# Probability-value products in four column quarters of the array, transposed back, in the second layer of a two-layer conditioned attention kernel

## The chip, the cores and the metric

The kernel runs on one core of one Trainium2 chip, in one launch. The metric is the device time of that launch in microseconds (us): all 64 sequences through both layers.

## The reference, cut to what matters

Sequences of 128 tokens and 512 features pass through two layers. The change is in the second, a softmax attention with 16 heads of 32 features, followed by a norm that a condition scales and shifts, a SiLU, an output product and a residual sum:

```python
xn = layer_norm(x, norm_w, norm_b)
q = (xn @ q_w + q_b).reshape(Bx, Tx, H, -1)          # H = 16, 32 features a head
k = (xn @ k_w + k_b).reshape(Bx, Tx, H, -1)
att = jnp.einsum('bnhl,bmhl->bnmh', q, k)
att = jax.nn.softmax(att + (1.0 - mask) * -1000000.0, axis=2)
v = ((xn @ v_w + v_b) * src_mask[:, :, None]).reshape(Bx, Tx, H, -1)
y = jnp.einsum('bnmh,bmhl->bnhl', att, v).reshape(Bx, Tx, Dx)
h = layer_norm(y, sb_norm_w, sb_norm_b) * (1.0 + scale) + shift
return x + (jax.nn.silu(h) @ out_w + out_b)
```

## The kernel before

The kernel is written for the engines directly: each engine has its own program, in the order in which the code writes it, and semaphores join them. `layer0` runs first (the other layer's attention), then `layer1`, which is the reference's second layer. `layer1` takes the sequences in 32 pairs, and each engine's `body(i, ...)` is one turn of a loop: it does the front part of pair i (projections, keys' and queries' scores, row maxima) and the back part of pair i-1 (weights, probability-value products, norm, gate, output product). So TensorE (PE), whose order is written by hand with `woven` (one step of each of two lists in turn), always has work of two pairs at hand. The eight PSUM banks are shared by name: `W_BANKS`, `Y_BANKS`, `Z_BANKS`, `O_BANKS`, `X_BANKS`, `S_BANKS`, `V_BANKS`, `QK_BANKS`.

The steps that the change and the prediction touch, in one turn of PE:

- `projected` (L439 to L441): keys, then queries; each feature block is 12 matmuls of 256 columns. Inputs are split into a high and a low part, so three matmuls stand for one product.
- `weight_scores` (L1417): scores again with the row maxima subtracted, into banks 4 to 7; ScalarE (ACT) makes `prob` from them with an exponential (`exps`, L1291). `prob[:, b, h, :]` has the keys on the partitions and the queries along the columns.
- `mixed` (L1427): for each of 16 heads `prob` is the stationary operand (128 columns) and `v` the moving one, 33 columns: 32 features and a column of ones, whose result is the sum of the probabilities. Both are float32, and the profile shows each such product as two weight loads and two matmuls. The result `y` has queries on partitions, as the norm wants it. In the profile's names it is `bank<-v,prob`.
- `end_outputs` (VectorE, DVE: L1169, L1174, L1179, L1182): reciprocal of the sums, product into `z`, statistics. GpSimd (POOL) makes the reciprocal deviation (L1073), `end_norm` (L1196) finishes `z`.
- `value_rows` (L430 to L432, 128x512, `xT`): 12 matmuls of 512 columns a sequence; `z_transposed` (L1376), `x_transposed` (L1366): 128x128 transposes of `z` and of the next pair's `xn`, which `x_high` (ACT, L1276) and `x_low` (DVE, L1143) split.
- `gate`, `tanh`, `end_silu`, `h_high`, `low_part` (ACT L1301, L1307, DVE L1201, ACT L1311, DVE L1205): from the transposed `z` to the operand of `out_rows` (L430 to L432 with `h_hi`, `h_lo`: 12 matmuls of 512 columns a sequence).
- `scores` (L1443): 16 matmuls a sequence into banks 0 to 3, in eight steps of two, from `stack`, in which SyncE's (SP) 24 DMAs of 128 KB (`restack`, L1034) put the high and low parts of keys and queries; `maxima` (DVE, L1160) takes the row maxima of each bank, `shift_row` (L1453) turns them, `shift_out` (ACT, L1315, L1317) sends them into `stack`.

`layer0` has one product that is laid out in column halves already, L922: two heads of 64 features share the array, each with 65 moving float32 columns. `tile_position=(0, DH * r)` there names the first column of the part of the array that the product uses.

Of the kernel before, what the change touches and what calls it, by code (L numbers as in the profile page):

```python
# [12 lines left out]
P = 128  # L13
PAIR = 2
# [941 lines left out]
def layer1(nc, ctx, sem, sb, ps, x1_d, out, xr, x_in, w_hi, w_lo, ident, bias_all, qk_bias,  # L956
# [4 lines left out]
    DV = DH + 1  # L961
# [11 lines left out]
    v = sb(ctx, "v1", [P, PAIR, H, DV])  # L973
# [27 lines left out]
        "shift0", "shift1", "w_ps", "prob", "y_ps", "p_sum", "y", "y_stats", "y_var", "y_var_eps", "y_rstd", "z",  # L1001
# [18 lines left out]
    def _(sp):  # L1020
        sp.wait_ge(s["rows_preset"], 1)

        def restack(i, first):
# [21 lines left out]
            sp.wait_ge(s["qk_lo"], seq(2 * C, i, 2 * C))  # L1045
            rows(0, Q_LO, 1)
# [77 lines left out]
    def _(dve):  # L1124
# [21 lines left out]
        def qk_low(i, n):  # L1146
            for c in range(C):
# [16 lines left out]
        def end_outputs(prev, b):  # L1164
            banks = Y_BANKS[b]
            dve.wait_ge(s["y_ps"], seq(PAIR, prev, b + 1))
            for j in range(2):
                a = ps[banks[j]][:, 0:HY * DV].rearrange("p (h d) -> p h d", h=HY)
                last = nc.vector.reciprocal(p_sum[:, b, HY * j:HY * j + HY], a[:, :, DH])  # L1169
            last.then_inc(s["p_sum"], 1)  # L1170
            dve.wait_ge(s["p_sum"], seq(PAIR, prev, b + 1))
            for j in range(2):
                a = ps[banks[j]][:, 0:HY * DV].rearrange("p (h d) -> p h d", h=HY)
                last = nc.vector.tensor_tensor(  # L1174
                    z[:, b, HY * DH * j:HY * DH * (j + 1)].rearrange("p (h d) -> p h d", h=HY), a[:, :, 0:DH],
                    p_sum[:, b, HY * j:HY * j + HY].unsqueeze(2).broadcast_to([P, HY, DH]), ALU.mult)
# [7 lines left out]
        def values(i, b, first):  # L1184
            dve.wait_ge(s["v_bias"], seq(1, i, 1))
            dve.wait_ge(s["v_ps"], seq(PAIR, i, b + 1))
            if not first:

                dve.wait_ge(s["y_ps"], seq(PAIR, i - 1, b + 1))
# [27 lines left out]
        nc.vector.memset(v[:], 1.0).then_inc(s["preset"], 1)  # L1217
# [6 lines left out]
        def body(i, first, more, last):  # L1224
            qk_low(i, 1)
            if not last:
                row_stats(i + 1, (i + 1) % RING)
            qk_low(i, 0)
            if not first:
                end_outputs(i - 1, 0)  # L1230
            if not last:
                norm(i + 1, (i + 1) % RING)
            if not first:
                end_norm(i - 1, 0)
                end_outputs(i - 1, 1)
# [16 lines left out]
            if not first:  # L1252
                end_add(i - 1, (i - 1) % RING, 0)
            maxima(i, 1, (2,))
            if not last:
                x_low(i + 1, 1)
            maxima(i, 1, (3, 0, 1))
# [15 lines left out]
    def _(act):  # L1273
# [13 lines left out]

        def exps(prev, b):
            for j in range(C):
# [3 lines left out]
                                     ACT.Exp).then_inc(s["prob"], 1)  # L1293

# [28 lines left out]
        def body(i, first, more, last):  # L1323
# [9 lines left out]
            if not first:  # L1333
                gate(i - 1, 0)
                tanh(i - 1, 0)
            if not first:
                h_high(i - 1, 0)
            if not first:
                gate(i - 1, 1)
                tanh(i - 1, 1)  # L1340
                h_high(i - 1, 1)
            if not last:
                x_high(i + 1, 0)
                x_high(i + 1, 1)
# [5 lines left out]
        exps(NP - 1, 1)  # L1350
        for b in range(PAIR):
            gate(NP - 1, b)
            tanh(NP - 1, b)
# [4 lines left out]
    def _(pe):  # L1358
# [62 lines left out]
        def mixed(prev, b):  # L1421


            pe.wait_ge(s["prob"], seq(PAIR * C, prev, C + 2 * (b + 1)))
            for h in range(H):
                j, a = h // HY, h % HY
                last = nc.tensor.matmul(ps[Y_BANKS[b][j]][:, a * DV:(a + 1) * DV], prob[:, b, h, :], v[:, b, h, :],  # L1427
                                        start=True, stop=True)
                yield
            last.then_inc(s["y_ps"], 1)  # L1430
# [26 lines left out]
        def body(i, first, more, last):  # L1457
# [12 lines left out]
            run(projected(i, 0, (0, 1)))  # L1470
            if first:
                run(projected(i, 0, (2, 3)))
            else:
# [61 lines left out]
```

## Time and profile before

| | |
|---|---|
| three runs | 2375.79, 2377.82, 2378.31 us, median 2377.82 |
| profiled execution | 2378.15 us; its span 2376.0 us |
| busy share of the span | PE 97%, weight loads (PEld) 87%, DVE 61%, ACT 35%, POOL 24% |
| one turn of `layer1`'s loop | 39.72 us (1619.98 to 1659.70) |

Times in the profile are counted from the span's start. PE's rows give the start of a matmul and a modelled duration that includes its way through the array, so that rows overlap; what a matmul costs the stream is the distance from its start to the next one's. PEld is the load of a stationary operand, which runs beside the matmul ahead of it. A row's bracket is the idle time ahead of it and what ended it.

### The profile page before, as it was taken

What the parts mean: (1) busy time and instruction counts of PE and PEld (TensorE: products, weight loads), DVE (VectorE), ACT (ScalarE), POOL (GpSimd) and SP (SyncE); (2) the same over time, 40 slices, a digit from 0 to 9 for tenths busy, and PEclk for the clock granted to TensorE, in tenths of its full rate; (3) what the DMA queues carried; (4) which work ended last, traced back from release to release, by engine and by line L of the source; (5) the groups of instructions that cost most, each with busy time, mean ns of one, the idle gap of its engine ahead of it and who ended that gap; (6) DMA issues with size and microseconds to landing.
All of it is one profiled execution on the core that took longest, in us unless ns stands there. A gap on an engine that the chain in (4) does not pass through costs nothing.

```text
span 2376.0 us, 44691 instructions
## 1 busy us (share of the span) xinstructions
PE 2316.1 (97%) x16182; PEld 2061.4 (87%) x16182; DVE 1459.6 (61%) x3249; ACT 822.1 (35%) x1893; POOL 574.3 (24%) x847
## 2 busy tenths in 40 slices
PE   7999999999999999969999999999999999999997
PEld 5888888888888888848898989898989898989896
DVE  4677777777777777653646465656565646464643
ACT  2233333333333333322333333333333333333332
POOL 0333333333333333231212121212122212222110
PEclk9999999999999999968999999999999999999997
DMA  7200000000001000004353535353434343434441
GB/s 244 80 36 35 35 35 35 35 35 35 35 35 35 33 34 35 32 32 109 89 124 90 124 90 122 92 121 94 120 95 118 96 117 94 118 95 118 97 109 41
DMA packets 90932, 187.14 MB, mean 79 GB/s; under 512 B 18708, under 2 KB 29394, under 8 KB 90904
## 3 DMA queue, kind: packets, MB, share of 16 engines
q1 hardware_dynamic: 88856, 186.23, 29.4%
q10 hardware_dynamic: 2048, 0.53, 0.1%
q8 instruction: 18, 0.29, 0.1%
q14 instruction: 10, 0.08, 0.0%
HBM read 51.81 MB, written 33.69 MB: 36 GB/s over the span
## 4 chain that ended last, share of the span: by engine, by line
PE 47%; ACT 4%; DVE 3%; issue 1%; SPq 1%; DMA 0%; DVEq 0%; POOL 0%; POOLq 0%
PE bank L1427 7%; PE bank L439 6%; PE bank L441 6%; PE bank L440 6%; PE bank L1417 5%; PE bank L431 4%; PE bank L432 4%; PE bank L430 4%; PE bank L1443 3%; ACT g L1301 2%; PE bank L1376 1%; PE bank L1366 1%; DVE top L1160 1%; DVE hs L1201 1%; ACT th L1307 1%
## 5 line engine op out<-in xcount | busy, mean ns | idle before, releaser
L439 PE MATMUL bank<-xT_hi,w_hi 128*128 128x256 f32 x1536 | 447.1, 291 | 2.6 <-DVE xT_lo L1143 1.4
L440 PE MATMUL bank<-xT_lo,w_hi 128*128 128x256 f32 x1536 | 447.6, 291 | 0.0
L441 PE MATMUL bank<-xT_hi,w_lo 128*128 128x256 f32 x1536 | 444.9, 290 | 0.0
L1152 DVE SCALAR_TENSOR_TENSOR parts<-bank,qk_bias,parts 128x256 fp32r<-128x256 f32 x256 | 112.2, 480 | 433.0 <-ACT parts L1284 433.0
L1427 PEld LDWEIGHTS bank<-v,prob 128*128 128x128 f32 x2048 | 317.6, 195 | 12.7
L430 PE MATMUL bank<-w_hi,xT_hi 128*128 128x512 f32 x768 | 322.2, 420 | 0.0
L432 PE MATMUL bank<-w_lo,xT_hi 128*128 128x512 f32 x768 | 322.1, 419 | 0.0
L431 PE MATMUL bank<-w_hi,xT_lo 128*128 128x512 f32 x768 | 319.9, 417 | 0.0
L439 PEld LDWEIGHTS bank<-xT_hi,w_hi 128*128 128x128 f32 x1536 | 292.4, 190 | 4.7 <-DVE xT_lo L1143 1.8
L440 PEld LDWEIGHTS bank<-xT_lo,w_hi 128*128 128x128 f32 x1536 | 293.8, 191 | 1.8
L441 PEld LDWEIGHTS bank<-xT_hi,w_lo 128*128 128x128 f32 x1536 | 293.4, 191 | 0.0
L1427 PE MATMUL bank<-v,prob 128*128 128x33 f32 x2048 | 293.3, 251 | 0.0
L430 PE MATMUL bank<-w_hi,h_hi 128*128 128x512 f32 x512 | 220.3, 430 | 3.6 <-DVE h_lo L1205 3.6
L1443 PEld LDWEIGHTS bank<-stack 98*128 98x128 f32 x1024 | 183.1, 194 | 45.1 <-DVE top L1160 23.0
L431 PE MATMUL bank<-w_hi,h_lo 128*128 128x512 f32 x512 | 215.4, 421 | 0.0
L432 PE MATMUL bank<-w_lo,h_hi 128*128 128x512 f32 x512 | 211.5, 413 | 0.0
L1284 ACT ACTIVATE parts<-bank,qk_bias 128x256 fp32r<-128x256 f32 x256 | 107.3, 470 | 288.5 <-PE bank L441 288.5
L787 ACT ACTIVATE k_exp<-bank,k_neg 128x128 f32<-128x128 f32 x256 | 72.8, 369 | 370.8 <-DVE k_neg L672 368.6
L1443 PE MATMUL bank<-stack 98*128 98x128 f32 x1024 | 178.8, 265 | 9.5 <-DMA stack<-parts 5.7
L1301 ACT ACTIVATE g<-bank,gains 128x128 f32<-128x128 f32 x256 | 96.2, 457 | 234.2 <-PE bank L1376 234.2
L1160 DVE TENSOR_REDUCE top<-bank 128x4 f32<-128x512 f32 x256 | 169.6, 682 | 7.5 <-PE bank L1443 7.3
L432 PEld LDWEIGHTS bank<-w_lo,xT_hi 128*128 128x128 f32 x768 | 145.1, 189 | 29.9
(163 smaller groups left out, 4078.6 us busy)
## 6 DMA issues: line engine op xcount, KB each, us to landing
stack<-parts SPq DMA_DIRECT2D x768, 128.0 KB
xr<-in_x SPq DMA_DIRECT2D x32, 512.0 KB, 3.5
x_between_layers<-x SPq DMA_DIRECT2D x64, 256.0 KB, 2.0
xr<-x_between_layers SPq DMA_DIRECT2D x32, 512.0 KB, 3.6
out<-y_out SPq DMA_DIRECT2D x64, 256.0 KB, 2.0
w_emb<-in_L_cond_W_emb SPq DMA_DIRECT2D x4, 1024.0 KB, 10.2
w_emb<-in_L_cond_emb_w SPq DMA_DIRECT2D x4, 1024.0 KB, 5.2
raw<-in_L_cond_Wq SPq DMA_DIRECT2D x1, 1024.0 KB, 5.4
```

What stands on the lines that cost most here:

```text
L430: yield nc.tensor.matmul(bank[:, :], a_hi[:, c, b, :], w_hi[:, m, c, :], start=(c == 0), stop=False)
L431: yield nc.tensor.matmul(bank[:, :], a_lo[:, c, b, :], w_hi[:, m, c, :], start=False, stop=False)
L432: yield nc.tensor.matmul(bank[:, :], a_hi[:, c, b, :], w_lo[:, m, c, :], start=False, stop=(c == C - 1))
L439: yield nc.tensor.matmul(dst, w_hi[:, m, c, fs], a_hi[:, c], start=(first and c == 0), stop=False)
L440: yield nc.tensor.matmul(dst, w_hi[:, m, c, fs], a_lo[:, c], start=False, stop=False)
L441: yield nc.tensor.matmul(dst, w_lo[:, m, c, fs], a_hi[:, c], start=False, stop=(c == C - 1))
L1152: nc.vector.scalar_tensor_tensor(parts[:, LO[n], c].rearrange("p b t -> p (b t)"), ps[QK_BANKS[n][c // 2]][:, at:at + PAIR * P], qk_bias[: ...
L1160: nc.vector.tensor_reduce(top[:, b, :].rearrange("p (a c) -> p a c", c=C)[:, :, j], ps[S_BANKS[j]][:, :].rearrange("p (h t) -> p h t", h=H ...
L1301: last = nc.scalar.activation(g[:, b, c, :], ps[Z_BANKS[b]][:, c * P:(c + 1) * P], ACT.Identity, scale=gains[:, 0, c, b:b + 1], bias=gains ...
L1417: last = nc.tensor.matmul(ps[W_BANKS[j]][:, a * P:(a + 1) * P], stack[0:K_SHIFTED, 1, a, j, b, :], stack[0:K_SHIFTED, 0, a, j, b, :], star ...
L1427: last = nc.tensor.matmul(ps[Y_BANKS[b][j]][:, a * DV:(a + 1) * DV], prob[:, b, h, :], v[:, b, h, :], start=True, stop=True)
L1443: last = nc.tensor.matmul(ps[S_BANKS[j]][:, a * P:(a + 1) * P], stack[0:K_SCORE, 0, a, j, b, :], stack[0:K_SCORE, 1, a, j, b, :], start=Tr ...
```

## The change

1. `mixed`: `v` (32 columns, no column of ones) becomes the stationary operand and `prob` the moving one, 128 columns. The four heads of a group go to the four column quarters of the array (`tile_position=(0, DH * a)`), and their results, features on partitions, fill one bank of a sequence. The sums come from 16 further products with `one_col`, a stationary operand whose column c is ones and whose other columns are zeros, so that the sums of 16 heads land in 16 rows of the second bank.
2. `copy_yT` (ACT) copies both results from PSUM into `prob`'s own place, and `turned` (PE) transposes them back in five 128x128 transposes a sequence. `end_outputs` then reads one bank of y and the sums from the other, with one reciprocal and one product in place of two each.
3. PE's order: all query blocks, then `mixed` of both sequences back to back, then `value_rows` woven with `turned`, then `z_transposed(0)`, the next pair's `x_transposed`, and all eight steps of the first sequence's scores; only behind them `z_transposed(1)` and the first `out_rows`, woven with the second sequence's scores. The second `out_rows` stands alone at the end.
4. ACT's order: `x_high` of the next pair stands ahead of `h_high(0)`, and four DMAs of the low query rows move from SP to ACT (`query_low_rows`). DVE's order: `values(0)` ahead of `end_norm(0)`, silu and low part of both sequences among the maxima.

```diff
-    v = sb(ctx, "v1", [P, PAIR, H, DV])
+    v = sb(ctx, "v1", [P, PAIR, H, DH])
+    one_col = sb(ctx, "one_col", [P, C, DH])
...
             rows(0, Q_HI, 0)
             rows(0, Q_HI, 2)
-            sp.wait_ge(s["qk_lo"], seq(2 * C, i, 2 * C))
-            rows(0, Q_LO, 1)
...
         def end_outputs(prev, b):
             banks = Y_BANKS[b]
             dve.wait_ge(s["y_ps"], seq(PAIR, prev, b + 1))
-            for j in range(2):
-                a = ps[banks[j]][:, 0:HY * DV].rearrange("p (h d) -> p h d", h=HY)
-                last = nc.vector.reciprocal(p_sum[:, b, HY * j:HY * j + HY], a[:, :, DH])
-            last.then_inc(s["p_sum"], 1)
+            nc.vector.reciprocal(p_sum[:, b, :].rearrange("p (c a) -> p c a", c=C),
+                                 ps[banks[1]][:, 0:P].rearrange("p (a r) -> p r a", a=HC)[:, 0:C, :])\
+                .then_inc(s["p_sum"], 1)
...
         def body(i, first, more, last):
-            qk_low(i, 1)
+            qk_low(i, 1, range(C))
             if not last:
                 row_stats(i + 1, (i + 1) % RING)
-            qk_low(i, 0)
-            if not first:
-                end_outputs(i - 1, 0)
+            qk_low(i, 0, range(C))
             if not last:
                 norm(i + 1, (i + 1) % RING)
             if not first:
+                end_outputs(i - 1, 0)
+            values(i, 0, first)
+            if not first:
                 end_norm(i - 1, 0)
                 end_outputs(i - 1, 1)
-                end_silu(i - 1, 0)
-            values(i, 0, first)
-            if not first:
-                end_norm(i - 1, 1)
-                low_part(i - 1, 0)
             values(i, 1, first)
             maxima(i, 0, (0,))
             if not first:
-                end_silu(i - 1, 1)
+                end_norm(i - 1, 1)
+                end_silu(i - 1, 0)
             maxima(i, 0, (1,))
             if not first:
-                low_part(i - 1, 1)
+                low_part(i - 1, 0)
             maxima(i, 0, (2,))
             if not last:
                 x_low(i + 1, 0)
             maxima(i, 0, (3,))
...
+        def query_low_rows(i):
+            act.wait_ge(s["qk_lo"], seq(2 * C, i, 2 * C))
+            for a in range(HC):
+                act.dma_start(f32(stack[DH:2 * DH, 0, a]),
+                              f32(parts[DH * a:DH * a + DH, Q_LO])).then_inc(s["stack"], 16)
...
+        def copy_yT(prev, b):
+
+            act.wait_ge(s["yT_ps"], seq(2 * PAIR, prev, 2 * b + 2))
+            nc.scalar.activation(prob[:, b, 0:C, :].rearrange("p h t -> p (h t)"), ps[Y_BANKS[b][0]][:, :],
+                                 ACT.Copy).then_inc(s["yT"], 1)
+            nc.scalar.activation(prob[:, b, C, :], ps[Y_BANKS[b][1]][:, 0:P], ACT.Copy).then_inc(s["yT"], 1)
...
         def mixed(prev, b):
 
-
             pe.wait_ge(s["prob"], seq(PAIR * C, prev, C + 2 * (b + 1)))
-            for h in range(H):
-                j, a = h // HY, h % HY
-                last = nc.tensor.matmul(ps[Y_BANKS[b][j]][:, a * DV:(a + 1) * DV], prob[:, b, h, :], v[:, b, h, :],
-                                        start=True, stop=True)
+            for c in range(C):
+                for a in range(HC):
+                    last = nc.tensor.matmul(ps[Y_BANKS[b][0]][DH * a:DH * a + DH, c * P:(c + 1) * P],
+                                            v[:, b, HC * c + a, :], prob[:, b, HC * c + a, :], start=True, stop=True,
+                                            tile_position=(0, DH * a))
+            last.then_inc(s["yT_ps"], 1)
+            for c in range(C):
+                for a in range(HC):
+                    last = nc.tensor.matmul(ps[Y_BANKS[b][1]][DH * a:DH * a + DH, 0:P], one_col[:, c, :],
+                                            prob[:, b, HC * c + a, :], start=(c == 0), stop=(c == C - 1),
+                                            tile_position=(0, DH * a))
+            last.then_inc(s["yT_ps"], 1)
...
-            run(projected(i, 0, (0, 1)))
+            run(projected(i, 0, range(C)))
+            if not first:
+                mixed(i - 1, 0)
+                mixed(i - 1, 1)
+            woven(value_rows(i, 0), () if first else turned(i - 1, 0))
+            woven(value_rows(i, 1), () if first else turned(i - 1, 1))
...
```

In PE's program, where the products stood between the matmuls of the query blocks and of the values in the turn before (end of the query blocks; the row with x6 holds the first sequence's last five and the second's first):

```order
L1427 MATMUL bank<-v,prob 128x33
L440 MATMUL bank<-xT_lo,w_hi 128x256
L441 MATMUL bank<-xT_hi,w_lo 128x256
L1427 MATMUL bank<-v,prob 128x33 x6
L430 MATMUL bank<-w_hi,xT_hi 128x512
L1427 MATMUL bank<-v,prob 128x33
L431 MATMUL bank<-w_hi,xT_lo 128x512
L1427 MATMUL bank<-v,prob 128x33
```

now 64 products stand in one block (L1445 those with `v`, L1451 the sums, L1462 `turned`):

```order
L441 MATMUL bank<-xT_hi,w_lo 128x256
L1445 MATMUL bank<-prob,v 32x128 [waits l1_prob]
L1445 MATMUL bank<-prob,v 32x128 x15
L1451 MATMUL bank<-prob,one_col 32x128 x16
L1445 MATMUL bank<-prob,v 32x128 [waits l1_prob]
L1445 MATMUL bank<-prob,v 32x128 x15
L1451 MATMUL bank<-prob,one_col 32x128 x16
L430 MATMUL bank<-w_hi,xT_hi 128x512 [waits l1_qk_lo]
L1462 MATMUL bank<-ident,prob 128x128 [waits l1_yT]
L431 MATMUL bank<-w_hi,xT_lo 128x512
L1462 MATMUL bank<-ident,prob 128x128
```

The products have left the rows between the projections; the transposes have come in among the values.

Later in the same turn, at the join of values, scores and output product, PE's program was:

```order
L1427 MATMUL bank<-v,prob 128x33
L431 MATMUL bank<-w_hi,xT_lo 128x512
L1376 MATMUL bank<-ident,z 128x128 x4
L1427 MATMUL bank<-v,prob 128x33 x5
...
L432 MATMUL bank<-w_lo,xT_hi 128x512
L1376 MATMUL bank<-ident,z 128x128 x4
L1443 MATMUL bank<-stack 128x128 x4
L430 MATMUL bank<-w_hi,h_hi 128x512
```

and is now (L1395 `z_transposed`, L1385 `x_transposed`, L1478 `scores`):

```order
L432 MATMUL bank<-w_lo,xT_hi 128x512
L1395 MATMUL bank<-ident,z 128x128 [waits l1_z]
L1395 MATMUL bank<-ident,z 128x128 x3
L1385 MATMUL bank<-ident,xn 128x128 [waits l1_y,l1_xn]
L1385 MATMUL bank<-ident,xn 128x128 x3
L1385 MATMUL bank<-ident,xn 128x128 [waits l1_y,l1_xn]
L1385 MATMUL bank<-ident,xn 128x128 x3
L1478 MATMUL bank<-stack 128x128 [waits l1_stack]
...
L1395 MATMUL bank<-ident,z 128x128 [waits l1_z]
L1395 MATMUL bank<-ident,z 128x128 x3
L430 MATMUL bank<-w_hi,h_hi 128x512 [waits l1_h_lo]
```

The first sequence's z is transposed behind the values of both sequences, no longer in the middle of the first's, and between it and the first output matmul stand eight transposes of the next x and 16 score matmuls.

ACT's program between the query parts and the end of the gates was (L1284 `qk_high`):

```order
L1284 ACTIVATE parts<-bank,qk_bias 128x256 x4
L1301 ACTIVATE g<-bank,gains 128x128 x4
L1307 ACTIVATE th<-g 128x512
L1311 ACTIVATE h_hi<-hs 128x4x128
L1301 ACTIVATE g<-bank,gains 128x128 x4
L1307 ACTIVATE th<-g 128x512
L1311 ACTIVATE h_hi<-hs 128x4x128
L1276 ACTIVATE xT_hi<-bank 128x4x128 x2
```

and is now:

```order
L1284 ACTIVATE parts<-bank,qk_bias 128x256 x4
L1304 ACTIVATE prob<-bank 128x512
L1306 ACTIVATE prob<-bank 128x128
L1291 DMA stack<-parts 32x1024 x4
L1304 ACTIVATE prob<-bank 128x512
L1306 ACTIVATE prob<-bank 128x128
L1314 ACTIVATE g<-bank,gains 128x128 x4
L1320 ACTIVATE th<-g 128x512
L1276 ACTIVATE xT_hi<-bank 128x4x128 x2
L1324 ACTIVATE h_hi<-hs 128x4x128
```

The copies and the four DMAs are new ahead of the gate, and the next x's high parts stand between the tanh and the high part of h.

## Rows read from the trace of the kernel before

**Rows 1.** The page: the span and the number of instructions.

```profile
span 2376.0 us, 44691 instructions
```

**Rows 2.** Windows, one turn: length, busy PE, PEld, DVE, ACT, POOL, clock, DMA.

```profile
1619.98:1659.70 39.72, 39.60 (x291) 36.30 (x290) 22.00 (x49) 14.29 (x32) 8.08 (x13) 1.00 0.44 107
```

**Rows 3.** Waits of PE's weight loads, 1400 to 2200: total, times, longest.

```profile
PEld bank L1443 <- DVE top L1160: 14.9, 40, 0.4
...
PEld bank L430 <- DVE h_lo L1205: 4.6, 20, 0.2
```

**Rows 4.** Timeline of PE: start, duration, instructions merged where alike.

```profile
1637.56 1.42 PE L1427 MATMUL bank<-v,prob 128*128 128x33 f32 x12
1638.81 0.48 PE L430 MATMUL bank<-w_hi,xT_hi 128*128 128x512 f32 x1
...
1639.27 0.48 PE L431 MATMUL bank<-w_hi,xT_lo 128*128 128x512 f32 x1
...
1645.69 0.40 PE L431 MATMUL bank<-w_hi,xT_lo 128*128 128x512 f32 x1
1645.93 0.39 PE L432 MATMUL bank<-w_lo,xT_hi 128*128 128x512 f32 x1
...
1647.32 0.27 PE L1366 MATMUL bank<-ident,xn 128*128 128x128 f32 x1
...
1647.66 0.27 PE L1366 MATMUL bank<-ident,xn 128*128 128x128 f32 x1
```

**Rows 5.** Timeline of PE in the first layer, products in column halves.

```profile
504.21 1.15 PE L922 MATMUL bank<-v,k_rows 128*64 128x65 f32 x32
505.30 0.50 PE L431 MATMUL bank<-w_hi,h_lo 128*128 128x512 f32 x1
505.63 0.39 PE L432 MATMUL bank<-w_lo,h_hi 128*128 128x512 f32 x1
```

**Rows 6.** Source line L922: shortest, median and longest matmul in ns.

```profile
L922 PE MATMUL bank<-v,k_rows x1024: 220/222/271, 86.6 to 1011.6; 128*64 128x65 f32 x171
```

**Rows 7.** Windows of L922 alone: matmuls begun (PE), loads begun (PEld).

```profile
504.20:504.31 0.11, 0.10 (x2) 0.10 (x4) 1.00 0.00 0
```

**Rows 8.** Timeline, second sequence from transposed z to output product.

```profile
1649.30 0.66 PE L1376 MATMUL bank<-ident,z 128*128 128x128 f32 x4
...
1650.00 1.50 ACT L1301 ACTIVATE g<-bank,gains 128x128 f32<-128x128 f32 x4 [1.33 <-PE bank L1376]
...
1652.20 0.69 DVE L1201 SCALAR_TENSOR_TENSOR hs<-th,g 128x512 f32<-128x512 f32 x1 [1.09 <-ACT th L1307]
...
1652.92 0.63 ACT L1311 ACTIVATE h_hi<-hs 128x512 fp32r<-128x512 f32 x1 [0.76 <-DVE hs L1201]
...
1653.46 1.07 ACT L1276 ACTIVATE xT_hi<-bank 128x512 fp32r<-128x512 f32 x2
...
1653.58 0.69 DVE L1205 TENSOR_TENSOR h_lo<-hs,h_hi 128x512 fp32r<-128x512 f32 x1
...
1654.38 0.45 PE L430 MATMUL bank<-w_hi,h_hi 128*128 128x512 f32 x1
```

**Rows 9.** Timeline of DVE: y to z, and three row maxima.

```profile
1645.34 0.28 DVE L1169 RECIPROCAL p_sum<-bank 128x8 f32<-128x8 f32 x2 [1.99 <-PE bank L1427]
...
1648.70 0.55 DVE L1196 TENSOR_SCALAR z<-z,mv_y,rstd_y 128x512 f32<-128x512 f32 x1
...
1657.78 1.88 DVE L1160 TENSOR_REDUCE top<-bank 128x4 f32<-128x512 f32 x3
```

**Rows 10.** Timeline of the queues of SP and ACT: issues.

```profile
1630.13 15.98 SPq L1034 DMA_DIRECT2D stack<-parts  x24
...
1658.37 0.52 ACTq L1317 DMA_DIRECT2D stack<-top_T  x1
```

**Rows 11.** The chain that ended last, first pair: last of its 24 DMAs.

```profile
1090.77 2.37 DMA stack<-parts
```

**Rows 12.** Windows, the last pair's products: PE, PEld, DVE, ACT, POOL, clock.

```profile
2343.00:2357.00 14.00, 14.00 (x68) 14.00 (x68) 2.66 (x10) 0.60 (x1) 1.01 (x4) 0.50 0.00 0
```

More of the change, by code:

```diff
@@ L1144, in x_low, with qk_low @@
                                     f32(xT_hi[:, :, b, :]), ALU.subtract).then_inc(s["xT_lo"], 1)
-        def qk_low(i, n):
-            for c in range(C):
+        def qk_low(i, n, chunks):
+            for c in chunks:
                 if c % 2 == 0:
@@ L1216, in _ @@
         row_stats(0, 0)
-        nc.vector.memset(v[:], 1.0).then_inc(s["preset"], 1)
+        nc.vector.memset(one_col[:], 0.0).then_inc(s["preset"], 1)
+        dve.wait_ge(s["preset"], 1)
+        for c in range(C):
+            last = nc.vector.memset(one_col[:, c, c:c + 1], 1.0)
+        last.then_inc(s["preset"], 1)
         nc.vector.memset(p_sum[:], 1.0).then_inc(s["out"], PAIR)
@@ L1252, in body @@
             if not first:
-                end_add(i - 1, (i - 1) % RING, 0)
-            maxima(i, 1, (2,))
+                end_silu(i - 1, 1)
             if not last:
                 x_low(i + 1, 1)
-            maxima(i, 1, (3, 0, 1))
+            if not first:
+                low_part(i - 1, 1)
+            maxima(i, 1, range(2, C))
+            if not first:
+                end_add(i - 1, (i - 1) % RING, 0)
+            maxima(i, 1, range(2))
             if not first:
@@ L1333, in body @@
             if not first:
+                copy_yT(i - 1, 0)
+            query_low_rows(i)
+            if not first:
+                copy_yT(i - 1, 1)
+            if not first:
                 gate(i - 1, 0)
                 tanh(i - 1, 0)
+            if not last:
+                x_high(i + 1, 0)
+                x_high(i + 1, 1)
             if not first:
                 h_high(i - 1, 0)
-            if not first:
                 gate(i - 1, 1)
@@ L1341, in body @@
                 h_high(i - 1, 1)
-            if not last:
-                x_high(i + 1, 0)
-                x_high(i + 1, 1)
             shift_out(i, 0)
@@ L1469, in body @@
                     weight_scores(i - 1, f // 2)
[L1470 to L1476 removed]
+            run(projected(i, 0, range(C)))
+            if not first:
+                mixed(i - 1, 0)
+                mixed(i - 1, 1)
+            woven(value_rows(i, 0), () if first else turned(i - 1, 0))
+            woven(value_rows(i, 1), () if first else turned(i - 1, 1))
             if not first:
                 z_transposed(i - 1, 0)
[L1479 to L1483 removed]
+            if not last:
+                run(x_transposed(i + 1, first))
             if first:
[L1485 to L1486 removed]
+                pe.wait_ge(s["preset"], 2)
+            scores0 = scores(i, 0, S_ORDER[0])
+            run(scores0)
             if not first:
                 z_transposed(i - 1, 1)
[L1489 to L1492 removed]
+            outputs0, scores1 = () if first else out_rows(i - 1, 0), scores(i, 1, S_ORDER[1])
+            woven(outputs0, scores1, 6)
             if not last:
@@ L1496, in body @@
             shift_row(i, 0)
-            woven(outputs1, scores1)
+            woven(outputs0, scores1)
+            if not first:
+                run(out_rows(i - 1, 1))
         bodies(pe, NP, body)
@@ L1503, in _ @@
         for b in range(PAIR):
-            run(mixed(NP - 1, b))
+            mixed(NP - 1, b)
+        for b in range(PAIR):
+            run(turned(NP - 1, b))
         for b in range(PAIR):
```

39 lines of the change are left out of this document (16 added, 23 removed).

## The prediction, made before the changed kernel ran

> **What bounds the kernel now.** The page first, for the span [rows 1]. Then windows laid over one turn of the second layer's loop, 39.72 us long, and the other turns are within 0.03 us of it but for the first and the last of 31 [rows 2]. PE is busy for 39.60 us of it at a clock of 1.00, DVE for 22.0, ACT for 14.3: PE's stream bounds the turn, and every matmul that leaves it or joins it counts, unless PE waits. The waits of its loads say how much it waits already: for DVE's row maxima 14.9 us in 20 turns and for the low part of h 4.6, so 1.0 us a turn [rows 3]. Not all of that is lost, since loads run ahead of the matmuls; I take 0.9 us a turn for it, and so 38.8 us of pure stream.
>
> **The old products.** A product with `v` costs what stands from start to start: six of them alone from 1637.56 to 1638.81, 0.21 us each; woven with a 512-column matmul the two take 0.46 us (1638.81 to 1639.27), where such a matmul alone takes 0.24 (1645.69 to 1645.93), so 0.22 us [rows 4]. It moves 33 columns only; its two loads of 128 columns set its price. 32 products a turn: 7.0 us go.
>
> **The new products.** 32 with `v` and 32 for the sums, each with two loads of 32 columns and two matmuls of 128 moving columns. No such form is in the trace. The nearest is the first layer's L922 in column halves, 65 moving float32 columns: 32 instructions, that is 16 products, over 1.15 us [rows 5]. Less the last one's own 0.22 us [rows 6] that is 0.93 us of starts, 0.058 us a product. Behind the block 0.15 us pass to the next start, and the matmul there takes 0.33 us where 0.24 is usual [rows 5]; with some 0.1 us for the entry the two ends cost 0.35 us. The price in quarters hangs on how many products are in flight. If four are, a product costs 0.058 x 128/65 x 2/4 = 0.057 us, 64 of them 3.7, with the ends 4.0 us. If only two are, as in halves, it is 0.114 us, and 7.65 us in all. Between these the window of L922's first 0.11 us decides for me: four loads have begun there, but two matmuls [rows 7]. [...] I take 4.0 us. What is not shown is that PE is supplied with 128 such instructions in a row at 0.03 us each; L922's run is of 32.
>
> [...]
>
> **The transposes.** Ten of 128x128 woven with the values. `x_transposed` is the same form in the same company: 0.34 us for transpose and matmul, 1647.32 to 1647.66, less 0.24 is 0.10 to 0.11 [rows 4]. They add 1.1 us.
>
> Pure stream: 38.8 - 7.0 + 4.0 + 1.1 = 36.9 us a turn. Were there no new waits, 31 turns would give 2.8 us each.
>
> **The wait that comes in.** It is the way from the transposed z of the first sequence to its output product. For the second sequence the trace has this way bare: z's transposes at 1649.30, gate at 1650.00, silu at 1652.20, high part at 1652.92, low part at 1653.58, first output matmul at 1654.38: 5.1 us, some 0.1 of it slack [rows 8]. In the new order ACT does both `x_high` (1.07 us [rows 8]) between the tanh and the high part. The silu runs meanwhile, so only about 0.3 us is added: 5.25 us. PE has in that time: 4 + 8 + 4 transposes and 16 score matmuls of the same width, 32 x 0.11 = 3.5 us, and some 0.15 us for `z_transposed(1)`, whose z stands behind the first row maximum on DVE. So PE waits 1.6 us ahead of the first output matmul. Behind it stand the second sequence's scores, woven: bank 2 waits for the maximum that DVE takes after the low part (0.60 us from maximum to maximum [rows 9], less one output matmul: 0.35 us), bank 3 for `x_low` and one more (1.2 us against some 0.9 of PE's work: 0.3 us). New waits: 1.6 + 0.15 + 0.65 = 2.4 us. Turn: 36.9 + 2.4 = 39.3 us, 0.4 less than now.
>
> **What is hidden, and by what.** Times from the end of the query blocks. (a) ACT: the two high parts end at 1.2 us; the first copy (0.54 us for 512 columns as half of `x_high`'s 1.07, 0.37 for 128 as a quarter of the gate's 1.50 [rows 8]) runs under the second sequence's products and ends at 3.2; four DMAs follow. Such an issue costs SP 15.98/24 = 0.67 us, ACT's of 8 KB 0.52 [rows 10]; I take 0.63, 2.5 us, and the second copy ends at 6.6. PE wants it at 4.0 + 3.5 + 0.2 = 7.7: 1.1 us of cover. (b) The first z: y is back at 5.8 us, and y to the end of z is 1648.70 + 0.55 - 1645.34 = 3.9 us [rows 9]: 9.8, where PE comes at 10.9. (c) The stack: SP's remaining eight query DMAs end soon after their last issue plus 2.4 us [rows 11], some 2 us ahead of the scores; all 24 share the same transfer engines (share 0.44 over the turn [rows 2]), so part of that goes. (d) The old half of the reciprocals and products on DVE is a small gain off the path.
>
> **Outside the turns.** In the first pair PE waits for the stack, and 4 of SP's 24 DMAs leave its queue: 4 x 0.63 = 2.5 us, 2 taken. Behind the last turn PE runs at half clock (0.50), and its 32 products fill some 13.8 of the 14 us [rows 12]. There the first y now comes later (7.3 + 0.4 + 1.1 = 8.8 us for products and transposes, against 6.9) and the second's way starts when DVE is through with the first: 8.8 + 2 x 3.9 = 16.6 us against 13.8 + 3.9 = 17.7: 1 us less.
>
> Sum, against the profiled execution's 2378.15 us (0.3 us above the median of the runs): 31 x 0.42 = 13, 2 and 1, together 16: **2362 us**.
>
> **Rivals.**
> - *Two in flight.* Place: `mixed`. [...] Price 3.65 us a turn: turn 42.95 us, 31 x 3.23 = 100 us more than now, and with the ends about 2475 us. It decides from 0.064 us a product on, where the turn's gain is gone. [...] Against it: four loads behind two matmuls. 0.17.
> - *The second copy is late.* If an issue on ACT takes twice as long while SP issues too, 2.5 us more use up the 1.1 of cover: PE waits 1.4 us a turn, 43 us in all, 2405 us. For it: both queues feed the same transfer engines, nearly full while the stack is laid (24 x 128 KB in 15.98 us). Against it: an issue alone on ACT is no dearer than on SP. 0.10.
> - *Other new waits are longer*, by 0.4 to 0.9 us: DVE has more to do between the scores and `end_add`. 2374 to 2390 us. 0.13.
> - *The wait is shorter than worked out*, by half: 2325 to 2345 us. It takes a gate that starts earlier than 0.7 us behind the transposes; the way of 5.1 us is measured, though. 0.10.
> - As worked out, with 0.5 us a turn either way: 2347 to 2377 us. 0.50.
>
> **Numbers.** A measurement of this kernel tells about 0.2% (4.8 us) from no change. Faster: 0.45 of the likeliest, 0.10 of the shorter wait, 0.01: 0.56. Same: 0.11, from the edges of the likeliest and of the longer waits. Slower: 0.33. The range runs from the shorter wait to the late copy, 2325 to 2405, and leaves out the two in flight; the likeliest's own is 2347 to 2377.
>
> **What would show it.** In the changed profile: L1445 and L1451 together 3.7 us a turn of starts (right) or 7.3 (two in flight); L1462 0.11 us each; a wait of PE for DVE's low part of h of about 1.6 us ahead of the output product; waits of L1478 for row maxima around 0.6 us; no wait of L1462 for ACT's copy, or 1.4 us if that is late; a turn of 39.3 us. A turn under 38.5 or over 40.0 us makes the prediction wrong.

## The result: 3.6% slower, and the profile after

| | before | after |
|---|---|---|
| time, median (us) | 2377.84 | 2463.29 (2462.26 to 2466.35) |
| ratio, 95% interval | | 1.0363 [1.0345, 1.0381] |
| profiled span (us) | 2376.0 [rows 1] | 2460.7 |
| one turn of the second layer (us) | 39.72 [rows 2] | 42.06 and 43.29, one after the other |
| PE's clock over such a turn | 1.00 [rows 2] | 0.92 and 0.88 |

The prediction was 2362 us (2325 to 2405), most likely faster. The time lies 101 us above it and outside the range.

The page of the kernel after, the span and PE's granted clock in 40 slices:

```profile
span 2460.7 us, 49634 instructions
...
PEclk9999999999999999878898998989898998989898
```

Windows, with the columns of [rows 2]. The first fence has the block of new products, the stretch from the last transposes of z to the first output product, and two turns in a row. The second has a high and a low stretch of the clock, laid edge to edge.

```profile
1587.57:1591.20 3.63, 3.63 (x130) 3.43 (x129) 1.79 (x4) 1.60 (x4) 0.00 (x0) 1.00 0.96 208
1601.29:1603.27 1.98, 0.65 (x5) 0.41 (x4) 1.89 (x4) 1.92 (x6) 0.00 (x0) 1.00 0.00 0
...
1587.57:1629.63 42.06, 40.62 (x366) 36.69 (x365) 22.07 (x45) 15.71 (x36) 7.34 (x13) 0.92 0.41 101
1629.63:1672.92 43.29, 41.96 (x365) 37.75 (x364) 22.07 (x45) 15.70 (x36) 7.33 (x13) 0.88 0.41 98
```

```profile
1604.34:1611.16 6.82, 6.82 (x25) 6.01 (x25) 3.77 (x7) 1.11 (x3) 0.00 (x0) 0.50 0.01 1
1611.16:1645.30 34.14, 32.83 (x338) 30.02 (x336) 17.22 (x38) 13.54 (x32) 7.33 (x13) 1.00 0.51 124
1645.30:1655.54 10.24, 10.22 (x32) 8.60 (x33) 5.67 (x10) 2.16 (x5) 0.00 (x0) 0.50 0.00 1
```

The answer is in the last column but two. The new products take 3.63 us, as hoped, and PE is idle in only one place, for some 1.3 us. But once in every turn its granted clock falls to 0.50 for 6.83 or 10.24 us (13.65 in the first). In the kernel before it stood at 1.00 in all these turns. Between 1120 and 2270 us the trace of after has 27 such low stretches in 27 turns, 235.5 us in all; that of before has none.

The timeline of PE around the wait shows what runs while the clock is low:

```profile
1598.03 0.60 PE L1395 MATMUL bank<-ident,z 128*128 128x128 f32 x4
...
1601.29 0.66 PE L1395 MATMUL bank<-ident,z 128*128 128x128 f32 x4
1603.27 0.50 PE L430 MATMUL bank<-w_hi,h_hi 128*128 128x512 f32 x1 [1.33 <-DVE h_lo L1200]
1603.88 0.44 PE L1478 MATMUL bank<-stack 98*128 98x128 f32 x2
1604.15 0.57 PE L431 MATMUL bank<-w_hi,h_lo 128*128 128x512 f32 x1
1604.51 0.53 PE L1478 MATMUL bank<-stack 98*128 98x128 f32 x2
1604.84 0.74 PE L432 MATMUL bank<-w_lo,h_hi 128*128 128x512 f32 x1
1605.37 0.52 PE L1478 MATMUL bank<-stack 98*128 98x128 f32 x2
1605.69 0.73 PE L430 MATMUL bank<-w_hi,h_hi 128*128 128x512 f32 x1
```

The first row has the transposes of the first sequence's z. Further down come those of the second, then nothing until DVE's low part of h is there, then the output products woven with the scores of the second sequence. From 1604.34 on an output product and its two score matmuls take 0.85 us from start to start (1604.84 to 1605.69), where the same group takes 0.46 in a kernel that keeps its clock (below). The waits of PE's weight loads, 1400 to 2200 us, beside those of [rows 3]:

```profile
PEld bank L430 <- DVE h_lo L1200: 28.2, 18, 1.6
PEld bank L1478 <- DVE top L1158: 6.7, 18, 0.4
```

The wait that the prediction worked out is there, 28.2/18 = 1.57 us a turn as its loads count it. PE itself, whose rows reach to the end of its last transpose, stands still for 1.33 us of it (the bracket above). Where two waits are compared below, it is by this idle time of PE. The wait had been priced at its own length. The two traces alone can't say whether the low clock comes from this wait, from the long run of narrow instructions, or from something else in the new order. The runs decide that.

### The profile page after: what moved, and what is told of

Its sections match the earlier page's. It is cut to its first block, busy times and chain, and to the rows that moved or that the text cites. A ratio compares the mean times of both kernels' runs of the same rounds, so it can differ in the third digit from the quotient of the medians.

```text
span 2460.7 us, 49634 instructions
## 1 busy us (share of the span) xinstructions
PE 2359.0 (96%) x18550; PEld 2079.4 (85%) x18550; DVE 1460.8 (59%) x3125; ACT 867.3 (35%) x2021; POOL 551.5 (22%) x847
## 4 chain that ended last, share of the span: by engine, by line
PE 48%; DVE 3%; ACT 2%; SPq 2%; issue 1%; DMA 1%; POOL 0%; DVEq 0%; POOLq 0%; ACTq 0%
PE bank L430 6%; PE bank L431 6%; PE bank L432 6%; PE bank L439 5%; PE bank L441 5%; PE bank L440 5%; PE bank L1436 5%; PE bank L1478 4%; PE bank L1445 2%; PE bank L1451 2%; SPq L1034 2%; PE bank L1462 1%; DVE top L1158 1%; ACT h_hi L1324 1%; PE bank L1385 1%
## 5 line engine op out<-in xcount | busy, mean ns | idle before, releaser
L440 PE MATMUL bank<-xT_lo,w_hi 128*128 128x256 f32 x1536 | 436.8, 284 | 0.0
L441 PE MATMUL bank<-xT_hi,w_lo 128*128 128x256 f32 x1536 | 434.0, 283 | 0.0
L430 PE MATMUL bank<-w_hi,h_hi 128*128 128x512 f32 x512 | 251.1, 490 | 43.8 <-DVE h_lo L1200 43.8
L1478 PEld LDWEIGHTS bank<-stack 98*128 98x128 f32 x1024 | 219.0, 257 | 46.1 <-DVE top L1158 12.5
L431 PE MATMUL bank<-w_hi,h_lo 128*128 128x512 f32 x512 | 245.5, 479 | 0.0
L432 PE MATMUL bank<-w_lo,h_hi 128*128 128x512 f32 x512 | 242.5, 474 | 0.0
L1478 PE MATMUL bank<-stack 98*128 98x128 f32 x1024 | 201.5, 325 | 11.4 <-DMA stack<-parts 9.8
L1090 POOL TENSOR_TENSOR xr<-xr,bias_all 128x512 f32 (+1 forms) x64 | 81.2, 1289 | 474.6 <-DVE top L1158 473.7
L1284 ACT ACTIVATE parts<-bank,qk_bias 128x256 fp32r<-128x256 f32 x256 | 107.3, 470 | 212.1 <-PE bank L441 212.1
L430 PEld LDWEIGHTS bank<-w_hi,h_hi 128*128 128x128 f32 x512 | 116.7, 228 | 68.9 <-DVE h_lo L1200 51.7
L430 PEld LDWEIGHTS bank<-w_hi,xT_hi 128*128 128x128 f32 x768 | 144.9, 189 | 35.6 <-issue 6.2
```

The source lines that it names most:

```text
L430: yield nc.tensor.matmul(bank[:, :], a_hi[:, c, b, :], w_hi[:, m, c, :], start=(c == 0), stop=False)
L431: yield nc.tensor.matmul(bank[:, :], a_lo[:, c, b, :], w_hi[:, m, c, :], start=False, stop=False)
L432: yield nc.tensor.matmul(bank[:, :], a_hi[:, c, b, :], w_lo[:, m, c, :], start=False, stop=(c == C - 1))
L440: yield nc.tensor.matmul(dst, w_hi[:, m, c, fs], a_lo[:, c], start=False, stop=False)
L441: yield nc.tensor.matmul(dst, w_lo[:, m, c, fs], a_hi[:, c], start=False, stop=(c == C - 1))
L1090: last = nc.gpsimd.tensor_tensor(xr[:, slot, b], xr[:, slot, b], bias_all[:, BO, :], ALU.add)
```

## The experiments

All were timed in three rounds against the kernel before on the same chip (2376.29 us for the first four, 2377.52 for the next four, 2376.76 for the last).

**1. Fill the wait with useless work.** Six 512-column matmuls stand between `z_transposed(1)` and the output products; they write a bank that the output products overwrite. Nothing else differs from after.

```diff
+        def fill(prev, n):
+            pe.wait_ge(s["g"], seq(PAIR, prev, 1))
+            for k in range(n):
+                nc.tensor.matmul(ps[O_BANKS[0]][:, :], w_hi[:, O, k % C, 0:P], w_hi[:, V, k % C, :],
+                                 start=True, stop=True)
...
                 z_transposed(i - 1, 1)
+                fill(i - 1, 6)
```

> The changed kernel with six matmuls of 512 columns (both operands weights, result thrown away in the bank that the first output product overwrites) between the transposes of the second z and the first output product, where PE stood idle for 1.6 us a turn. Theory (the idle 1.6 us makes the clock fall to half for 7 to 10 us of each turn): work of the same length in its place keeps the clock at 1.00, the turn falls from 42.65 to 39.3 to 39.6 us, the kernel to 2355 to 2375 us. Rival A (the column quarters, little of the array in use, make it fall): no change, 2455 to 2470 us. Rival B (the row of narrow matmuls ahead of the wait, transposes and scores, makes it fall): no change either, 2455 to 2470 us.

Measured: 2354.95 us, ratio to before 0.9913 [0.9897, 0.993]. 186 useless matmuls make the kernel after 108 us faster. No low stretch is left between 1120 and 2270 us. A turn, from windows, and the waits of the loads:

```profile
1587.00:1626.17 39.17, 39.04 (x374) 34.92 (x378) 22.08 (x45) 15.71 (x36) 7.32 (x13) 1.00 0.45 108
```

```profile
PEld bank L1478 <- DVE top L1158: 15.7, 42, 0.4
PEld bank L430 <- DVE h_lo L1200: 8.0, 21, 0.4
```

39.17 us is the turn of the new order at full clock; the prediction said 39.3. So the low clock costs after 42.68 - 39.17 = 3.5 us a turn (42.68 is the mean of the two turns above), times 31 = 109 us, and that is all of the difference between these two runs.

**2. Shorten the wait instead.** The first sequence's z is made earlier: its products stand ahead of the last query block, their transposes back ahead of the second sequence's products, `z_transposed(0)` between the two value blocks; DVE and ACT follow in the same order (`norm`, SiLU and the low part of the first sequence ahead of its row maxima, `h_high(0)` ahead of both `x_high`).

```diff
...
-            run(projected(i, 0, range(C)))
+            run(projected(i, 0, (0, 1, 2)))
             if not first:
                 mixed(i - 1, 0)
+            run(projected(i, 0, (3,)))
+            if not first:
+                run(turned(i - 1, 0))
                 mixed(i - 1, 1)
-            woven(value_rows(i, 0), () if first else turned(i - 1, 0))
-            woven(value_rows(i, 1), () if first else turned(i - 1, 1))
+            run(value_rows(i, 0))
             if not first:
                 z_transposed(i - 1, 0)
+            woven(value_rows(i, 1), () if first else turned(i - 1, 1))
```

> The changed kernel with the idle stretch removed by order: the first sequence's products stand ahead of the last query block, its transposes ahead of the second's products, z_transposed(0) between the values of the two sequences, DVE and ACT reordered to suit. The same work and four changes of array mode a turn instead of two. Theory (idle stretch): no wait of over 0.5 us is left, the clock stays at 1.00, the turn is 37.3 to 38.0 us, the kernel 2300 to 2325 us. Rival A (quarters): the clock still falls, 3.3 us a turn more, 2400 to 2430 us. Rival B (narrow matmuls in a row): their row of transposes and scores is the same but for four, so 2400 to 2430 us too.

Measured: 2436.70 us, ratio 1.025 [1.0222, 1.0277]. Its expectation did not come true, because my order had made another wait of the same length. PE's timeline and its loads' waits:

```profile
1636.13 0.49 PE L430 MATMUL bank<-w_hi,h_hi 128*128 128x512 f32 x1
1637.93 0.44 PE L1477 MATMUL bank<-stack 98*128 98x128 f32 x2 [1.30 <-DVE top L1158]
```

```profile
PEld bank L1477 <- DVE top L1158: 33.6, 28, 1.6
```

The low part of h is in time, but it and the norm now stand ahead of all row maxima on DVE, and the second score step waits for that of bank 2. PE stands still from about 1636.6 to 1637.9, and the clock falls at 1638.91. So the run says nothing against the theory and little for it, but one thing more: 22 of its 27 turns between 1120 and 2270 us have a low stretch (41.9 or 43.3 us long, from block to block), and every sixth has none and takes 38.91, with the same wait in it. PE's idle time is 1.30 us in each. The window over such a stretch, and the waits in it:

```profile
1690.11:1761.79 71.68, 69.37 (x697) 62.82 (x695) 37.91 (x81) 29.92 (x69) 15.40 (x26) 1.00 0.47 118
```

```profile
PEld bank L1477 <- DVE top L1158: 1.9, 2, 1.6
```

**3. A wait in the kernel before.** No part of the change, only a wait of TensorE ahead of the first output product for a useless product of 1280 columns on GpSimd, which starts with the second sequence's z.

```diff
+                pool.wait_ge(s["z"], seq(PAIR, i - 1, PAIR))
+                rows = bias_all[:].rearrange("p k d -> p (k d)")[:, 0:1280]
+                nc.gpsimd.tensor_tensor(late_out[:, 0:1280], rows, rows, ALU.mult).then_inc(s["late"], 1)
...
             run(islice(scores0, 2))
+            if not first:
+                pe.wait_ge(s["late"], seq(1, i - 1, 1))
             woven(outputs0, scores0)
```

> The kernel before, with one wait added: PE waits ahead of the first output product for a GpSimd product of 1280 columns that starts when the second z is ready (an estimated 2.6 us, so PE idles for about 1.7 us a turn where it came at once before). No column quarters. Theory (idle stretch): the clock falls in each turn, turn 39.75 + 1.7 + 3.3 = 44.7 us, kernel about 2530 us, mean clock about 0.93. Rivals A and B: only the wait itself, turn 41.4 us, kernel about 2430 us, mean clock 0.98.

Measured: 2506.27 us, ratio 1.0544 [1.0527, 1.0562]. The waits of PE, then windows over the low stretch that begins 0.2 us behind the wait, and over the high one up to the next:

```profile
PE bank L430 <- POOL late_out L1120: 32.8, 19, 1.7
```

```profile
1574.71:1581.54 6.83, 6.83 (x23) 5.86 (x24) 3.90 (x6) 1.60 (x3) 0.00 (x0) 0.50 0.00 0
1581.54:1619.08 37.54, 35.81 (x271) 33.41 (x270) 18.82 (x44) 12.68 (x29) 10.77 (x14) 1.00 0.47 113
```

Quarters, copies and the new order are all absent, and the clock falls once a turn (26 times) as it does in after. A wait of 1.7 us is enough for it. The time is below the 2530 us expected: the 26 low stretches are 163.9 us in all, shorter than the 27 of after. Of the 130 us over before, the wait's own length explains at most 31 x 1.7 = 53; the rest, some 2.5 us a turn, goes with the low clock.

**4. The new order with the old products.** `mixed` is that of before (33 columns, 64 instructions for both sequences in a row), with no copies and no transposes back; all else is after.

```diff
-            for c in range(C):
-                for a in range(HC):
-                    last = nc.tensor.matmul(ps[Y_BANKS[b][0]][DH * a:DH * a + DH, c * P:(c + 1) * P],
-                                            v[:, b, HC * c + a, :], prob[:, b, HC * c + a, :], start=True, stop=True,
-                                            tile_position=(0, DH * a))
...
+            for h in range(H):
+                j, a = h // HY, h % HY
+                last = nc.tensor.matmul(ps[Y_BANKS[b][j]][:, a * DV:(a + 1) * DV], prob[:, b, h, :], v[:, b, h, :],
+                                        start=True, stop=True)
...
-            woven(value_rows(i, 0), () if first else turned(i - 1, 0))
-            woven(value_rows(i, 1), () if first else turned(i - 1, 1))
+            run(value_rows(i, 0))
+            run(value_rows(i, 1))
```

> The changed kernel's order with the old probability-value products (prob stationary, 33 moving columns, 7.0 us a turn, no quarters, no copies, no transposes back). Theory (idle stretch): the wait of 1.6 us ahead of the first output product is the same, so the clock falls: stream 38.8 + waits 2.4 + clock 3.3 = 44.5 us a turn, kernel about 2525 us. Rival A (quarters): no fall, 41.2 us a turn, about 2425 us. Rival B (narrow matmuls in a row): falls too, about 2525 us.

Measured: 2635.95 us, ratio 1.1087 [1.1051, 1.1123]; dearer than expected, with 48 low stretches where after has 27. Windows over two low stretches of one turn, over the block of old products, and from the last transposes of z to the first output product:

```profile
1606.12:1612.94 6.82, 6.82 (x26) 6.05 (x26) 0.36 (x3) 0.00 (x0) 1.00 (x4) 0.50 0.81 169
1623.18:1630.01 6.83, 6.83 (x24) 5.74 (x24) 3.43 (x6) 0.90 (x2) 0.00 (x0) 0.50 0.01 1
1600.74:1609.35 8.60, 8.60 (x66) 8.60 (x65) 3.76 (x11) 0.84 (x2) 1.00 (x4) 0.81 0.99 222
1619.79:1621.77 1.98, 0.66 (x5) 0.42 (x5) 1.89 (x4) 1.98 (x6) 0.00 (x0) 1.00 0.00 0
```

The second begins 1.4 us behind the wait's end (1621.77); the one of after shown above begins 1.1 us behind its. The first begins in the middle of the block of old products, where PE waits for nothing. That was new, and run 9 takes it up.

**5 and 6. Half the filler, and another filler.** Run 5 is run 1 with three matmuls; run 6 is run 1 with twelve transposes of 128 columns in place of the six matmuls of 512.

```diff
-                fill(i - 1, 6)
+                fill(i - 1, 3)
```

```diff
-                nc.tensor.matmul(ps[O_BANKS[0]][:, :], w_hi[:, O, k % C, 0:P], w_hi[:, V, k % C, :],
-                                 start=True, stop=True)
+                nc.tensor.transpose(ps[O_BANKS[0]][:, 0:P], z[:, 1, P * (k % C):P * (k % C + 1)], ident[:])
```

> The kernel after with only three 512-column filler matmuls (0.72 us) in the wait of 1.55 us ahead of the first output product, so that about 0.8 us of wait stays in a turn. Idle-stretch theory (the clock falls because TensorE stands for over 1.5 us in this place): a turn still falls only sometimes or not at all, since 0.8 us is near the waits that before had without a fall; 2355 to 2410 us. If any remaining wait in this place is enough: 2440 to 2465 us. If the filler's gain had come from something else than the clock (the order of the queues), 2355 us again with the clock low as in the kernel after.

> As the six-matmul filler, but the wait is filled with twelve 128-column transposes (some 1.3 us at 0.11 us each) instead of six 512-column matmuls. If it is only the standing still that lowers the clock, this is as good as the 512-column filler: 2350 to 2365 us. If narrow work counts little, so that the stretch of transposes, scores and filler still reads as slack, the falls stay in most turns: 2430 to 2475 us.

Measured: 2359.53 us, 0.9925 [0.9909, 0.9942], with half the filler, and 2356.89 us, 0.9912 [0.9895, 0.9929], with the transposes. Each has a single low stretch between 1120 and 2270 us. The waits of the loads for the low part of h, first in run 5, then in run 6:

```profile
PEld bank L430 <- DVE h_lo L1200: 22.5, 21, 1.1
```

```profile
PEld bank L430 <- DVE h_lo L1200: 5.4, 21, 0.3
```

Waits of 1.1 us by the loads, 13.4/21 = 0.6 of them idle for PE itself, were followed by a low stretch once in 28 turns. And work of 128 columns holds the clock here as well as work of 512.

**7. The mended order.** Run 2, with six of the first sequence's twelve output matmuls ahead of the second's first score step, so that DVE has time for its row maxima.

```diff
             outputs0, scores1 = () if first else out_rows(i - 1, 0), scores(i, 1, S_ORDER[1])
+            run(islice(outputs0, 6))
             woven(outputs0, scores1, 6)
```

> The order with the norms and the z transposes pulled ahead, and now six of the twelve output products of the first sequence ahead of the first score step of the second, so that the maxima of bank 2 (ready 1.8 us after the first output product) are met by 1.5 us of products. Idle-stretch theory: waits of 0.3 us or less, a turn of 37.4 us at full clock throughout, so 2376 - 31 x 2.3 = 2305 us (2290 to 2330). If the new order itself (quarters, narrow work in a row) lowers the clock without a wait: 2400 us or more, with falls in most turns.

Measured: 2305.6 us (2304.07 to 2306.24), ratio to before 0.9699 [0.9683, 0.9715]: 3.0% faster than before and 6.4% faster than after, with no filler. A turn from windows, the two waits that last longest in a turn, and PE's timeline where run 2 stood still:

```profile
1607.00:1644.51 37.51, 37.49 (x375) 33.76 (x368) 21.84 (x46) 15.82 (x36) 7.68 (x13) 1.00 0.46 113
```

```profile
PEld bank L1477 <- DVE top L1158: 14.3, 43, 0.3
PEld bank L1394 <- DVE z L1191: 4.3, 21, 0.2
```

```profile
1621.97 0.62 PE L1394 MATMUL bank<-ident,z 128*128 128x128 f32 x4
1622.39 0.50 PE L430 MATMUL bank<-w_hi,h_hi 128*128 128x512 f32 x1
1622.72 0.39 PE L431 MATMUL bank<-w_hi,h_lo 128*128 128x512 f32 x1
...
1624.46 0.45 PE L431 MATMUL bank<-w_hi,h_lo 128*128 128x512 f32 x1
1624.75 0.33 PE L1477 MATMUL bank<-stack 98*128 98x128 f32 x2
1624.92 0.45 PE L432 MATMUL bank<-w_lo,h_hi 128*128 128x512 f32 x1
```

PE is busy for 37.49 of 37.51 us. An output product and its two score matmuls take 0.46 us here (1624.46 to 1624.92). 39.72 - 37.51 = 2.2 us a turn, times 31 = 68 of the 72 us gained over before.

**8. A shorter wait in the kernel before.** Run 3 with 768 columns on GpSimd.

> The kernel before with the GpSimd product of 768 instead of 1280 columns (some 1.6 us instead of 2.7) that TensorE awaits ahead of the first output product: a wait of about 0.75 us a turn instead of 1.8. If a wait of this length lowers the clock as the long one did: 2376 + 31 x 3.3 = 2480 us (2455 to 2490). If it doesn't: only the wait itself, 31 x 0.7, 2390 to 2405 us with the clock at full level.

Measured: 2389.39 us, ratio 1.0054 [1.0037, 1.007]. PE's waits, and one turn:

```profile
PE bank L430 <- POOL late_out L1120: 17.4, 20, 0.9
```

```profile
1600.00:1640.13 40.13, 39.26 (x292) 36.48 (x292) 22.10 (x49) 14.32 (x32) 9.95 (x14) 1.00 0.43 105
```

No low stretch between 1120 and 2270 us. The added wait of 0.87 us makes the turn 40.13 - 39.72 = 0.41 us longer; the small waits of [rows 3], 1.0 us a turn, are gone from its list and pay the rest. Twice that wait, in run 3, cost 130 us instead of 12.

**9. The old products with the wait filled.** Run 4 with the six filler matmuls of run 1.

> The new order with the old 33-column products (no quarters, no copies and transposes back), which showed two low stretches in a turn: one beginning inside the 8.4 us block of 64 old products in a row, one after the wait ahead of the first output product. Here the six-matmul filler covers that wait. If the block in itself lowers the clock (TensorE is at work all the time there, but with 33 columns an instruction): one low stretch a turn stays, in the block, 2635 - 31 x 3.3 = 2535 us (2510 to 2560). If both stretches had their root in the wait: no low stretch, 2440 to 2480 us.

Measured: 2531.49 us, ratio 1.0652 [1.0635, 1.067], 104 us less than run 4, with 25 low stretches in 25 turns. Windows over the low stretch and over the block of old products:

```profile
1617.16:1623.98 6.82, 6.82 (x28) 6.34 (x28) 0.88 (x3) 0.00 (x0) 1.00 (x4) 0.50 0.89 183
1612.31:1621.39 9.09, 9.09 (x66) 9.09 (x65) 3.76 (x11) 0.84 (x2) 1.00 (x4) 0.77 0.99 221
```

The two low stretches of run 4 have two causes. The filler takes away the one behind the wait, and the one that begins 4.9 us into the block stays. There TensorE is at work throughout, but with 33 columns an instruction; the kernel before has the same products woven with 256- and 512-column matmuls, and it has no low stretch between 1120 and 2270 us.

## Why the prediction was wrong

By its own steps:

- **The old products: right.** "Its two loads of 128 columns set its price": the loads of L1427 fill all of the 1.25 us in which those six products start, and an instruction with 33 moving columns takes 0.10 us there, no less than a transpose with 128 [rows 4]. The kernel before, a window of the loads alone (length, busy time and loads, clock, DMA):

```profile
1637.56:1638.81 1.25, 1.25 (x13) 1.00 0.96 207
```

- **The new products: right, a little too dear.** "I take 4.0 us", with four in flight. Measured 3.63 us for 128 instructions, 0.057 us a product, and that includes the ends, for which the prediction had added 0.35 us. PE was supplied with 128 such instructions in a row. The two-in-flight rival (7.65 us) is excluded. But no run shows that four loads behind two matmuls [rows 7] tell four in flight from two: that step was my estimate, and the 4.0 us rested on it. What decides is in the windows of L1445 alone: four matmuls have begun by 1587.60, no fifth by 1587.70, and eight by 1587.73.

```profile
1587.56:1587.60 0.04, 0.03 (x4) 0.03 (x5) 1.00 1.32 308
1587.56:1587.70 0.14, 0.13 (x4) 0.13 (x8) 1.00 1.08 263
1587.56:1587.73 0.17, 0.16 (x8) 0.16 (x12) 1.00 0.89 217
```

  Four matmuls start within 0.04 us, and the next four some 0.11 us behind them (32 in 0.90 us). That is what one transpose of 128 columns takes in the same trace (four from 1598.03 to 1598.46 us). In this sense four are in flight. The rows do not name the two parts of a product, so the order in which the parts start is not shown.
- **The transposes back: right.** 1591.54 to 1591.88 us is one of them with its 512-column matmul (0.34), and the rest of the turn agrees.
- **The way from z to the output product: right.** "5.25 us"; measured 5.24, from the first sequence's transposes at 1598.03 to the product at 1603.27.
- **The wait that comes in: right in length, wrong in price.** "PE waits 1.6 us ahead of the first output matmul"; the loads wait 1.57, PE stands still for 1.33. Run 1's turn has 15.7/21 = 0.75 us for row maxima, against 0.65 said for the two new ones.
- **The second copy: in time.** The lists of waits have none of L1462 for ACT.
- **"Turn: 36.9 + 2.4 = 39.3 us": here the prediction failed.** The sum took every matmul of the turn at the full clock of [rows 2]. With the clock kept, the turn measures 39.17 (run 1), and the whole kernel 2355 us against the 2362 predicted. The turn comes this close partly by luck: the new products took 0.37 us less than the sum had for them, so the rest of the turn took some 0.24 us more. With the wait of 1.57 us left empty, the clock falls, and 3.5 us of the turn's remaining work come on top. No rival had this either: "other new waits are longer" priced longer waits by their length alone.

What the runs show of the cause: filling the wait, with wide or narrow work, brings the time back (1, 5, 6); a wait of 1.7 us in the kernel before lowers the clock in every turn too and costs 130 us, without any part of the change (3); a wait half as long leaves the clock alone and costs 12 us, less than its length (8); and an order without the wait keeps all that the quarters give (7). The quarters alone did no harm to the clock: in runs 1 and 7 their block stands at 1.00 in every turn between 1120 and 2270 us, where the old products in a row did lower it (9).

The accounts close. 42.68 - 39.72 = 2.96 us a turn, times 31 = 92, where 85.5 were measured. By PE's first projection of each turn the two traces differ so: the second turn begins at 1097.98 instead of 1100.78 us, 2.8 earlier (1.8 of it already at the first pair's first projection, 1065.37 for 1067.16); from there to the start of the last turn it takes 1286.96 instead of 1194.89 us, 92.1 more; and the last turn with all that follows takes 75.7 instead of 80.3 us, 4.6 less. Together that is the spans' difference, 84.7 us. For the two ends the prediction had 3 us of gain, and they gave 7.4.

The hint was in the trace of before: [rows 12] show the tail at 0.50 and [rows 2] a turn at 1.00, so the clock moves within this kernel. I priced the tail at its low clock but took that of the turns for granted while adding to them the longest wait that they had ever held; the longest in [rows 3] is 0.4 us. The trace of before even has a wait of about the new one's size, behind its last turn (2337.68 to 2339.54), and the clock falls to 0.50 within it. The timeline's row behind that wait, and the window of the low stretch:

```profile
2339.54 3.68 PE L1417 MATMUL bank<-stack 99*128 99x128 f32 x16 [1.86 <-DMA stack<-top_T]
2338.32:2369.04 30.72, 23.18 (x97) 21.64 (x98) 7.63 (x20) 7.88 (x17) 1.75 (x6) 0.50 0.00 1
```

Open: why the same wait is followed by a low stretch in five turns of six in run 2 and by none in the sixth; why one stretch lasts 6.83 and the next 10.24 us in after (in the turns from 1400 to 1900 us the long ones begin within 0.1 us of the wait's end, the short ones 1.1 us behind it); and how much idle time of PE the turn can bear between the 0.9 us of run 8 and the 1.3 of after. Run 3 waited for 1.7 us; whether 1.3 would lower the clock in the kernel before too, no run tests. Nor is it shown that 0.9 us would do no harm elsewhere: run 5's one low stretch followed an idle time of 0.6 us.

## What to carry to other kernels

Where TensorE's stream sets the time and its trace shows both levels of the clock, a new wait may not be priced by its length alone: in this kernel a wait of 1.6 us (1.3 of it idle for PE) in a turn of 40 cost 3.5 us more, in the work behind it. So when a change cuts work from TensorE, look for the place where the cut turns into a wait, and spend the saved time there: move an independent step into it or, as a quick test of whether the clock is the cause, put useless matmuls there. And when an order is changed on one engine, redo the sums for the engine that it waits for: run 2 and run 7 differ by where six matmuls stand, and by 131 us.

## What the runs showed that I had not expected

- Useless work pays: 1.4 us a turn of it in run 1 made the kernel after 4.4% faster (2463.29 to 2354.95 us).
- The clock fell around idle times of PE of 1.3 us (after, 2) and 1.7 us (3) in turns of 40 us that were otherwise nearly full, and, but for one turn of run 5, not after 0.6 us (5) or 0.9 us (8). What ties the clock to them, no run shows.
- The clock also fell with no wait at all, in a block of 32 products of 33 columns, 64 instructions (9; its recorded expectation says 64 products), but not in a block of 128 instructions in column quarters with 128 columns each (1, 7).
- Products in column quarters, two instructions each, ran four in flight at 0.028 us an instruction, 32 in 0.90 us from 1587.57 to 1588.47, as PE's timeline of after has them:

```profile
1587.57 1.08 PE L1445 MATMUL bank<-prob,v 128*32 128x128 f32 x32
1588.47 1.06 PE L1451 MATMUL bank<-prob,one_col 128*32 128x128 f32 x32
```

- Their price follows the clock. In run 5 the block behind the last turn stands in a low stretch (2326.72 to 2333.55), and 32 instructions take 1.71 us from start to start, twice as long:

```profile
2328.36 1.94 PE L1445 MATMUL bank<-prob,v 128*32 128x128 f32 x32
2330.07 1.94 PE L1451 MATMUL bank<-prob,one_col 128*32 128x128 f32 x32
```
